# Moving the logits of two query tiles by 128 columns, and reordering TensorE's work around the turns, in a fused decoder layer

## What is computed

```
x = x + attn(layernorm(x))     # cumulative sums of low-rank (64) projections: bilinear, inverse and trilinear ranks
x = x + xattn(layernorm(x), ctx)
x = x + ffn(layernorm(x))

xattn(h, mem):                 # mem: 77 context rows per sequence
    n = rmsnorm(h) * norm_w;  v = concat([n, mem])
    logits = (n @ q_w.T) @ (v @ k_w.T).T / 16, causal over the tokens, the context always visible
    a = sigmoid(h @ gate_w.T + gate_b)
    return (1 - a) * h + a * (softmax(logits) @ v)

ffn(h): q = fp4 quantise and dequantise in blocks of 16
    g = silu(q(h) @ q(w_gate).T) * (q(h) @ q(w_up).T);  return q(g) @ q(w_down).T      # 704 hidden
```

## Time and profile before

| | |
|---|---|
| median of 3 runs | 540.25 us (540.16 to 540.3) |
| the profiled execution's own time | 540.15 us |
| its span in the trace | 538.4 us |
| PE busy | 521.7 us (97%), 3084 matmuls |
| PE's weight loads busy | 454.9 us (84%) |
| DVE busy | 451.3 us (84%) |
| ACT busy | 342.8 us (64%) |
| POOL busy | 410.9 us (76%) |
| DMA | 13.86 MB, 26 GB/s on the mean |

### The profile page before, as it was taken

One profiled execution on the slowest core, in us unless ns is written; L12 is line 12 of the kernel. 1 busy time (PEld: TensorE's weight loads), 2 busy tenths in 40 slices (PEclk: granted clock), 3 DMA queues, 4 the chain that ended last, 5 costly groups with the idle time before them and its releaser, 6 DMA issues.

```text
span 538.4 us, 10582 instructions
## 1 busy us (share of the span) xinstructions
PE 521.7 (97%) x3084; PEld 454.9 (84%) x3084; DVE 451.3 (84%) x1118; ACT 342.8 (64%) x811; POOL 410.9 (76%) x639
## 2 busy tenths in 40 slices
PE   8898899999999999999999998999999999999996
PEld 5777788888888888888888886998899999999996
DVE  3798889777897867969589689998899999999886
ACT  3555844737437474563675767787788888888763
POOL 4267939859589497697787937889988888888854
PEclk9999999999999999999999999999999999999999
DMA  8720500000000000000000000000000000000001
GB/s 234 214 80 2 162 0 2 0 2 1 1 1 0 2 0 2 2 0 1 1 2 2 0 1 1 11 19 19 13 22 22 21 20 19 19 19 19 21 19 50
DMA packets 16130, 13.86 MB, mean 26 GB/s; under 512 B 3883, under 2 KB 15839, under 8 KB 16095
## 3 DMA queue, kind: packets, MB, share of 16 engines
q1 hardware_dynamic: 16095, 13.43, 8.0%
HBM read 9.23 MB, written 4.19 MB: 25 GB/s over the span
## 4 chain that ended last, share of the span: by engine, by line
PE 72%; DVE 15%; issue 6%; ACT 4%; POOL 1%; DVEq 0%; ACTq 0%; POOLq 0%
PE ps L1062 16%; PE ps L1064 15%; PE ps L1063 15%; PE ps L1265 10%; PE ps L1453 3%; PE ps L1253 2%; PE ps L1263 2%; DVE parts L1541 2%; PE ps L1184 1%; PE ps L1401 1%; DVE X L1606 1%; PE ps L1313 1%; DVE gz L1627 1%; DVE xn_sums L1571 1%; DVE st L1612 1%
## 5 line engine op out<-in xcount | busy, mean ns | idle before, releaser
L1062 PE MATMUL ps<-keys_h,nT_h 128*128 128x256 f32 (+6 forms) x272 | 85.8, 315 | 1.4 <-DVE keys_l L1541 1.0
L1063 PE MATMUL ps<-keys_l,nT_h 128*128 128x256 f32 (+6 forms) x272 | 83.1, 306 | 0.0
L1064 PE MATMUL ps<-keys_h,nT_l 128*128 128x256 f32 (+6 forms) x272 | 83.1, 305 | 0.0
L1062 PE MATMUL ps<-parts,xq_parts 128*128 128x512 f32 (+1 forms) x192 | 74.6, 388 | 0.0
L1064 PE MATMUL ps<-parts,xq_parts 128*128 128x512 f32 (+1 forms) x192 | 72.0, 375 | 0.0
L1063 PE MATMUL ps<-parts,xq_parts 128*128 128x512 f32 (+1 forms) x192 | 71.8, 374 | 0.0
L1265 PE MATMUL ps<-V,probT 128*128 128x256 f32 x288 | 67.4, 379 | 0.0
L774 ACT ACTIVATE prob<-ps,nbias 128x205 f32<-128x205 f32 (+7 forms) x32 | 25.7, 803 | 61.9 <-DVE nbias L1633 61.8
L1265 PEld LDWEIGHTS ps<-V,probT 128*128 128x128 f32 x288 | 54.6, 190 | 7.6
L1062 PEld LDWEIGHTS ps<-keys_h,nT_h 128*128 128x128 f32 x272 | 51.3, 189 | 5.8 <-DVE keys_l L1541 1.2
L1063 PEld LDWEIGHTS ps<-keys_l,nT_h 128*128 128x128 f32 x272 | 51.3, 189 | 3.2
(11 more groups left out here) (236 smaller groups left out, 1594.1 us busy)
## 6 DMA issues: line engine op xcount, KB each, us to landing
X<-in_x_dram SPq DMA_DIRECT2D x8, 512.0 KB, 4.6
out_dram<-X SPq DMA_DIRECT2D x32, 128.0 KB, 1.7
early<-in_L_ffn_w_down_dram SPq DMA_DIRECT2D x1, 704.0 KB, 6.9
early<-in_L_ffn_w_gate_dram SPq DMA_DIRECT2D x1, 640.0 KB, 4.5
early<-in_L_ffn_w_up_dram SPq DMA_DIRECT2D x1, 640.0 KB, 5.8
ctx_rows<-in_ctx_dram SPq DMA_DIRECT2D x1, 308.0 KB
early<-in_L_attn_Winv_dram SPq DMA_DIRECT2D x1, 256.0 KB, 3.8
early<-in_L_attn_WQ_dram SPq DMA_DIRECT2D x1, 256.0 KB, 3.6
```

Of the source, the lines that this page charges most:

```text
L1062: mm(o, wh, mh, start=start, stop=False, **kw)
L1063: mm(o, wh, ml, start=False, stop=False, **kw)
L1064: return mm(o, wl, mh, start=False, stop=stop, **kw)
```

## The change

On all engines the logits of tiles 3 and 7 lie 128 columns further in PSUM: they begin at column 178 and end at 768 and 1280. The number of columns is the same; the pieces are now 334 and 256 columns, and 334, 512 and 256. PE's products, DVE's maximum and ACT's exponential use the new places. On PE, projection tiles 2 and 3 in stages 4 and 7 and the gates in stages 4 and 6 are made ahead of the turn of their stage instead of behind it. In the feed-forward part, steps 2 and 3 turn their gated tile behind piece 0 of the next tile's products, and ACT copies it behind that piece's silu.

```
--- before.py
+++ after.py
@@ -72,6 +72,7 @@
     NT_BANK = (0, 1, 6, 7)
     KEYS_BANK = (1, 6)
     FIRST_GATES = [[], [], [], [], [4, 5], [], [6, 7], [], [], []]
+    MOVED = (3, 7)
     GATES = [[0, 1], [2, 3], [], [], [4, 5], [], [6, 7], [], [], []]
 
     with ExitStack() as ctx:
@@ -771,7 +772,8 @@
                 if i >= 2:
                     act.wait_ge(s_prob_turned, b * CPB + chunk0[i - 1])
                 L = (i + 2) * P
-                a.activation(prob[:, i % 2, CTX0:L], flat[:, CTX0:L], ACT.Exp, bias=nbias[:, i:i + 1],
+                moved = P if i in MOVED else 0
+                a.activation(prob[:, i % 2, CTX0:L], flat[:, CTX0 + moved:L + moved], ACT.Exp, bias=nbias[:, i:i + 1],
                              scale=1.0, accum_out=rsum[:, i:i + 1]).then_inc(s_exp, 1)
 
             def turn_tile(b, i):
@@ -1004,7 +1006,7 @@
                     x_high(n + 2, u)
                 if left >= 4:
                     norm3(n + 4, u, parts)
-                if done >= 2:
+                if done >= 4:
                     down_turn(n - 2, u)
                 if left >= 3:
                     x_magnitude(n + 3)
@@ -1013,6 +1015,8 @@
                     h_magnitude(n, first=True)
                 if left >= 1:
                     silu(n + 1, 0)
+                if done in (2, 3):
+                    down_turn(n - 2, u)
                 if left == 1:
                     silu(n + 1, 1)
                 if done >= 1:
@@ -1224,12 +1230,13 @@
                 if i == TPB - 1:
                     pe.wait_ge(s_gz, b * TPB + TPB)
                 q = slice(i * P, (i + 1) * P)
-                L = (i + 2) * P
-
-                for lo in [v for v in (CTX0 - PAD, 512, 1024) if v < L]:
+                first = CTX0 - PAD + moved
+                L = (i + 2) * P + moved
+
+                for lo in [v for v in (first, 512, 1024) if v < L]:
                     hi = min(L, (lo // 512 + 1) * 512)
                     diag = hi == L
-                    t = slice(lo - CTX0 + PAD, hi - CTX0 + PAD)
+                    t = slice(lo - first, hi - first)
                     for k in range(KD):
                         last = mm_parts(flat[:, lo:hi], (nT_h[:, k, q], nT_l[:, k, q]), (keys_h[:, k, t], keys_l[:, k, t]),
                                         start=(k == 0), stop=(k == KD - 1 and not diag), skip_group_check=diag)
@@ -1331,8 +1338,15 @@
                         logits_tile(b, i)
                     if is_first(b) and i == 0:
                         keep_warm(FIRST_WARM, 4)
+                    if more and i == 4:
+                        proj_tiles(b * 2 + 2, (2, 3))
                     if more and i == 5:
                         y_half(b + 1, 0)
+                    if more and i == 7:
+                        proj_tiles(b * 2 + 3, (2, 3))
+                    if i in (4, 6):
+                        for t in GATES[i]:
+                            gate_tile(b, t)
                     if not more and i == TPB:
                         turn_tile(b, TPB - 1, (0, 1))
                         pe.wait_ge(s_w_h, 2 * KD)
@@ -1344,10 +1358,6 @@
                     elif 1 <= i <= TPB and not (is_first(b) and i == 2):
                         turn_tile(b, i - 1)
                     if more:
-                        if i == 4:
-                            proj_tiles(b * 2 + 2, (2, 3))
-                        if i == 7:
-                            proj_tiles(b * 2 + 3, (2, 3))
                         if i == TPB:
                             turn_nrm(b + 1, 0)
                             turn_nrm(b + 1, 1)
@@ -1356,7 +1366,7 @@
                         if not is_first(b):
                             turn_nrm(b, 2)
                             turn_nrm(b, 3)
-                    if not (i == 0 and is_first(b)):
+                    if i == 1 or (i == 0 and not is_first(b)):
                         for t in GATES[i]:
                             gate_tile(b, t)
                     if i == 1 and is_first(b):
@@ -1473,10 +1483,12 @@
                 gate_up(n, u, 2)
                 if left >= 2:
                     x_turn(n + 2)
-                if done >= 2:
-                    h_turn(n - 2, first=(done == 2))
+                if done >= 4:
+                    h_turn(n - 2)
                 if left >= 1:
                     gate_up(n + 1, 1 - u, 0)
+                if done in (2, 3):
+                    h_turn(n - 2, first=(done == 2))
                 if left == 1:
                     gate_up(n + 1, 1 - u, 1)
                     gate_up(n + 1, 1 - u, 2)
@@ -1630,7 +1642,8 @@
             def max_tile(b, i):
                 n = b * TPB + i
                 ve.wait_ge(s_logits, n + 1)
-                v.tensor_reduce(nbias[:, i:i + 1], flat[:, CTX0:(i + 2) * P], AX.X, ALU.max, negate=True).then_inc(s_neg_max, 1)
+                moved = P if i in MOVED else 0
+                v.tensor_reduce(nbias[:, i:i + 1], flat[:, CTX0 + moved:(i + 2) * P + moved], AX.X, ALU.max, negate=True).then_inc(s_neg_max, 1)
 
             def mix_tile(b, i):
                 n = b * TPB + i
```

7 lines of the change are left out of this document (2 added, 5 removed).

## The result

The kernel after took 536.55 us (median of 4 runs, 535.89 to 538.04), the kernel before beside it 540.2 (539.66 to 540.3): ratio 0.9937, 95% interval 0.992 to 0.9954. The forecast was 536.8.

What follows compares the result with a forecast made beforehand. The prediction took PE to bound the kernel nearly everywhere, with DVE or ACT setting the end in places. From 540.15 us it took 1.7 + 1.65 + 0 = 3.35, giving 536.8, range 535.1 to 538.5.

Steps and rivals of the forecast that it cites:

- The bound: Whole kernel: PE is busy nearly the whole span, 72% of the chain of waits is PE, 15% DVE.
- Part 1: Logits of tiles 3 and 7: the new column split saves 0.21 us a tile, 8 tiles, 1.7 us.
- rival C: Logits of tiles 3 and 7: columns alone count, the new split saves nothing; 538.5 us, chance 0.04.
- E: Whole change: PE's stalls only shift and the column split saves nothing, so no change; 540.2 us, chance 0.04.
- PE is not kept waiting just behind any of them: Logits of tiles 3 and 7: no PE wait follows the 8 tiles, so each 0.21 us counts.
- Part 2: Projections and gates ahead of the turns: DVE's scan starts 0.55 us earlier in three batches, 1.65 us.
- the two gaps: PE's waits for DVE's x1 and low parts, 0.33 and 0.28 us; first removed whole, some 0.06 left.
- The last batch: Stages 4 and 6 only make gates earlier there; the chain is PE alone, gain 0.
- rival B: Projections and gates moved: POOL or ACT sets x1's or the low parts' time, gain lost; 538.5 us, chance 0.11.
- Part 3: Feed-forward fill, first two gated tiles turned later: gain 0, as DVE frees PSUM bank 0 only at 335.40.
- nothing here makes PE idle longer, so no term is taken for the clock: Whole kernel: granted clock stays at 1.00, its upper level of 2.4 GHz; no time added.
- Rival D: Feed-forward fill: late copy of turned tile 0 delays DVE's low part, 4.4 us slower; 541.2 us, chance 0.02.

Runs made afterwards that it cites:

- no_ffn_move: The changed kernel with feed-forward steps 2 and 3 put back as before the change; 536.67 us, ratio 0.9922.
- after_again: The changed kernel run once more, unchanged, for the spread of its executions; 536.63 us, ratio 0.9931.

## Why the prediction was right, point by point

**The bound.** PE issues useful work nearly always and waits for DVE at few places. This held: the distance fell by the stalls and the cheaper split of columns taken out.

**Part 1, 1.7 us.** The new split saves 0.23 in tile 7, near what was computed (0.21). Rivals C and E are out: the 256-wide products that now stand in the place of the 128-wide ones, ahead of the mask, cost 0.12 us as elsewhere, so the place carries no cost. What holds a 128-wide product at 0.10 was not tested. The rule that would give rival C's time is stated in the Trainium skill (TensorE: Matmul & The Clock Gate, section Back-to-back issue gap) for a single product in isolation, which the prediction left out. But "PE is not kept waiting just behind any of them" failed in two places. In batch 0 the turn of the input behind logits 3 now waits for DVE's low part of the keys, which was just in time before (PE in order of time, `no_ffn_move`):

```profile
60.38 1.06 PE L1158 MATMUL ps<-ident,xn_sums 128*128 128x128 f32 x8 [0.26 <-DVE keys_l L1549]
```

That turn starts 34.71 us behind the first product for `y` before and 34.73 here: tile 3 saves nothing there. And alone, tile 3's saving went into the stage-1 wait. Singly the part was worth 1.24.

**Part 2, 1.65 us.** 0.50 for each of three batches where 0.55 was forecast; the two gaps went as worked out, to the usual extra of a first product (0.09 to 0.1). The 0.55 was five times 0.11; the prediction's own row starts give 140.20 - 139.72 = 0.48 for the five transposes ahead of the projections. The last batch, put at nothing, gave 0.2 more. Of rival B the place was wrong (neither ACT nor POOL released a late x1 or low part), its kind was right: a wait outside the stretch that I had read, at stage 1, took 0.9 us back when the order was changed alone (0.58 and 0.32 in the table), and POOL had its part in that through DVE's stretched addition. The terms were worked out from DVE and PE in stages 4 to 6; the prediction does not ask whether what runs earlier there meets anything in stages 0 and 1 of the next batch.

**Both.** The two parts were forecast as a sum of 3.35 and gave 3.2, near it since with both made the stage-1 wait was back at its old length. That is partly luck, in how DVE's and POOL's instructions happen to lie against each other: the gains measured singly add up to 1.95, by which the time would have been 538.2.

**Part 3, nothing.** The working held: DVE's first gated chunk of step 3 starts 19.39 us behind the third turned input before (334.99 - 315.60) and 19.38 in `after_again`, so PE's place there is DVE's, and PE's wait for ACT became waits for POOL and DVE. Two things were missed. The seventh turned input comes 0.15 us later. And "nothing here makes PE idle longer, so no term is taken for the clock" was the step that failed: two waits of 0.89 and 0.45 with a step's work between them became 1.08 and 0.60 with only two transposes between them, and the granted clock fell in 3 of 22 executions, for 1.6 us in each of the two that were profiled. The median of four runs does not show it. Rival D did not occur: DVE's low part starts 17.73 us behind that turned input before and 17.72 in `after_again`.

## What to carry to other kernels

A gap that is closed on the busiest engine is worth its length only if the next wait behind it has room: read on to the same point of the next iteration, and take a chain of waits apart from its last one. Where two parts of a change shift the same waits, their sum is no forecast of both, and each alone may look worth little. A reordering that brings two short waits of TensorE close together can cost clock in some executions, even if the work done is on time; here 3 of 22.

## What the runs showed of the hardware that was not expected

A float32r product of 128 columns costs 0.10 us and one of 256 columns 0.12; the wider one costs that in the gates and at the end of a tile alike. A VectorE and a GpSimd instruction with two SBUF inputs each take turns: 0.42 us became 0.97 where VectorE's came 0.06 us behind the start of GpSimd's, and GpSimd's next one 0.92 instead of 0.74. The addition ended 1.01 to 1.03 us behind the start of GpSimd's wherever it began 0.06 to 0.59 us behind it. The granted clock fell to 0.50 behind two waits of 1.08 and 0.60 us in one execution of the changed kernel and stayed at 1.00 behind waits of the same length in another; of all executions with this order 3 of 22 have the lower mean clock, and what tells them apart stays open.
